# Graph message passing on one core: the column ramp of the one-hot compare moves from a PSUM bank to SBUF

## The reference, cut to what matters

```python
# nodes: 12500 x 64, edges: 200000; row, col = source and destination of each edge (col is sorted)
msg_in = concatenate([nodes[row], nodes[col], edge_features], axis=-1)   # 64 + 64 + 32
messages = relu(msg_in @ mW1 + mb1) @ mW2 + mb2
aggregated = segment_sum(messages, col, num_segments=12500)
upd = relu(concatenate([nodes, aggregated]) @ uW1 + ub1) @ uW2 + ub2
out = layernorm(nodes + upd)
```

## Time and profile before

| | |
|---|---|
| time, median of 3 runs | 1975.1 us (1973.61 to 1975.39) |
| time of the profiled execution | 1975.1 us |
| its span, first to last instruction | 1973.4 us |
| PE busy | 1430.3 us, 72% |
| POOL busy | 1437.8 us, 73% |
| DVE busy | 1066.4 us, 54% |
| ACT busy | 782.8 us, 40% |
| mean granted TensorE clock | 0.802 of full speed |

### The profile page before, as it was taken

The page is one execution under the profiler, slowest core; times in us unless marked ns, Lnnn a source line. Parts: engine busy times, 40 slices in busy tenths (PEclk is TensorE's granted clock), DMA queues, the critical chain, the costliest instruction groups (busy, mean ns, idle before and its releaser), DMA issues.

```text
span 1973.4 us, 41684 instructions
## 1 busy us (share of the span) xinstructions
PE 1430.3 (72%) x10176; PEld 1296.3 (66%) x10176; DVE 1066.4 (54%) x4914; ACT 782.8 (40%) x4005; POOL 1437.8 (73%) x1528
## 2 busy tenths in 40 slices
PE   5777676677676767777676778777777777776776
PEld 5776666666666766666676667666666666675664
DVE  3565455545545545544455555555555656555563
ACT  3353333333333333433333444444444444444442
POOL 1677777777777777777777777777777777777773
PEclk8897878877777787777868787888888787878887
DMA  9833233223322322332232323333322333232321
GB/s 215 241 98 82 79 79 82 80 76 82 82 79 77 84 81 79 78 84 78 77 79 79 80 77 81 79 81 79 81 79 78 81 82 81 77 81 79 81 78 44
DMA packets 173605, 171.32 MB, mean 87 GB/s; under 512 B 72074, under 2 KB 135954, under 8 KB 173474
## 3 DMA queue, kind: packets, MB, share of 16 engines
q0 software_dynamic: 48480, 99.38, 19.4%
q1 hardware_dynamic: 111394, 64.27, 11.7%
q10 hardware_dynamic: 13698, 7.28, 1.6%
HBM read 154.44 MB, written 16.34 MB: 87 GB/s over the span
## 4 chain that ended last, share of the span: by engine, by line
POOL 69%; issue 23%; DMA 3%; PE 2%; POOLq 1%; DVE 1%; SPq 0%; ACT 0%; DVEq 0%; ACTq 0%
POOL ag L314 69%; PE bank L477 1%; DMA src_table<-ag 1%; DMA dst_table<-picks 1%; DMA xc<-x_t 1%; POOLq L233 1%; PE bank L353 0%; POOLq L311 0%; PE bank L368 0%; DVE hid L416 0%; DVE own_x L290 0%; DMA ag<-src_table,slot_idx 0%; DMA own_columns<-resid 0%; PE bank L749 0%; DVE picks L498 0%
## 5 line engine op out<-in xcount | busy, mean ns | idle before, releaser
L314 POOL DMA_INDIRECT ag<-src_table,slot_idx x1515 | 1431.2, 945 | 509.8 <-issue 460.1
L368 PE MATMUL bank<-oh,hid 128*128 128x96 f32 x3128 | 540.1, 328 | 356.5 <-ACT hid L394 353.0
L368 PEld LDWEIGHTS bank<-oh,hid 128*128 128x128 f32 x3128 | 481.7, 235 | 414.0 <-ACT hid L394 401.4
L416 DVE TENSOR_TENSOR hid<-bank,ag 128x512 f32<-128x512 f32 (+1 forms) x391 | 263.7, 674 | 770.6 <-DMA ag<-src_table,slot_idx 752.3
L394 ACT ACTIVATE hid<-hid 128x512 f32<-128x512 f32 x343 | 215.8, 629 | 983.5 <-DVE hid L416 983.5
L353 PE MATMUL bank<-picked,picks 128*128 128x128 f32 x3128 | 567.6, 339 | 7.0 <-DMA picks<-edge_t 6.2
L353 PEld LDWEIGHTS bank<-picked,picks 128*128 128x128 f32 x3128 | 506.5, 245 | 11.9 <-issue 9.2
L302 ACT ACTIVATE own_x<-xc 64x4 uint8 x3072 | 328.3, 189 | 0.0
L290 DVE COPY own_x<-xc 64x4 uint8 x3072 | 305.2, 183 | 12.0
L402 DVE TENSOR_TENSOR oh<-bank,rel 128x384 f32<-128x384 f32 x391 | 217.9, 557 | 54.2 <-issue 25.5
L383 ACT ACTIVATE picks<-bank 96x512 f32<-96x512 f32 x391 | 224.5, 574 | 22.9 <-DMA dst_table<-picks 22.2
(11 more groups left out here) (62 smaller groups left out, 411.3 us busy)
## 6 DMA issues: line engine op xcount, KB each, us to landing
picks<-edge_t SPq DMA_DIRECT2D x391, 64.0 KB
ag<-src_table,slot_idx POOLq DMA_INDIRECT x1515
picked<-dst_table SPq DMA_DIRECT2D x391, 48.0 KB
src_table<-ag SPq DMA_DIRECT2D x25, 256.0 KB, 4.3
dst_table<-picks SPq DMA_DIRECT2D x17, 256.0 KB, 4.5
xc<-x_t ACTq DMA_DIRECT2D x8, 400.0 KB, 15.3
resid<-x_rows SPq DMA_DIRECT2D x24, 128.0 KB
out<-resid ACTq DMA_DIRECT2D x24, 128.0 KB
```

The source lines that it names most:

```text
L314: pool.indirect_dma_start(out=ag[:, k, j * DH:(j + 1) * DH], out_offset=None, in_=src_table, in_offset=bass.IndirectOffsetOnAxis(ap=slot_i ...
L368: nc.tensor.matmul(ps_a[q][:, 0:WIN], hid[:, q, j * DH:(j + 1) * DH], oh[:, r, j * WIN:(j + 1) * WIN], start=(j == 0), stop=(j == TPG - 1))
L416: dve.tensor_tensor(hid[:, q, 0:w], ps_h[q][:, 0:w], ag[:, k, 0:w], ALU.add).then_inc(s_pre, 1)
```

## The change

`iota` gets an SBUF tensor of its own, 96 float32 numbers in each partition, where it was the head of PSUM bank 6. L1059 writes it there, and L402 reads it there. Nothing else of the program is edited, and each engine's instructions stand in the same order as before.

```diff
@@ -92,6 +92,7 @@
         iota_i = sb("iota_i", [P, WIN], i32)
+        iota = sb("iota", [P, WIN])
         ones_bf = sb("ones_bf", [P, P], bf16)
@@ -152,7 +153,6 @@
         ps_h, ps_o, ps_a = banks[0:2], banks[2:4], banks[4:6]
-        iota = banks[6][:, 0:WIN]
@@ -1056,7 +1056,7 @@
             dve.wait_ge(s_iota, 3)
-            dve.tensor_copy(iota, iota_i[:, :])
+            dve.tensor_copy(iota[:, :], iota_i[:, :])
             dve.tensor_copy(trash_f[:, :], trash_i[:, :])
```

## The result

| | before | changed |
|---|---|---|
| median of 4 runs | 1974.89 us (1973.61 to 1975.39) | 1991.68 us (1991.02 to 1992.42) |
| ratio | | 1.0086, 95% interval 1.0068 to 1.0104 |
| profiled execution, its span | 1975.1, 1973.4 us | 1988.31, 1986.6 us |

The change costs 17 us. The forecast was a loss of 45.5 us, 2020.6, and its range began at 2003.0. The direction and the place are as forecast, the size is less than half. The profiled execution lies 3.4 us under the median of the runs, so what follows accounts for 13.2 us and not for 17.

What follows compares the result with a forecast made beforehand. POOL's back-to-back gathers were taken to bound the kernel. L402's shorter duration counted 0 and its 228 collisions 45.5 us, so 1975.1 + 45.5 = 2020.6 us, range 2003 to 2040.

Steps and rivals of the forecast that it cites:

- What bounds the kernel: POOL's back-to-back gathers, 1515 periods of 1.248 us; only a longer POOL instruction or gap changes the time, one for one.
- L402's own duration: DVE's compare L402, 557 ns, gets 0 to 21 ns shorter, 0 to 8.2 us in all; taken as 0.
- What two SBUF inputs do to POOL: A two-SBUF-input DVE instruction running 126 ns into a gather holds POOL to its end: 228 hits, 45.5 us.
- Rival A: No collision from L402, since overwriting the tensor being read is what holds POOL; 1975.1 us, chance 0.06.
- the overlay: The collision rule laid over the trace before, for each of 391 L402: 228 hits and 45.5 us.
- Phases: L402's starts against POOL's gathers stay as they are when delays feed back, since L290 too goes with POOL.
- rival C: Delays avoid each other: lagging POOL meets L402 between read points, all 156 regular hits become misses; 1996.1 us, chance 0.08.
- The prediction's own table of shifts: Loss if L402 moves against POOL: 35.8 us for 104 ns earlier, 58.0 for 104 later, 79.4 for 200.
- the regular 156 hits: L402 starting 950 to 1000 ns after a gather's start, behind L290, all hit; 24.5 us together.
- B: Faster: DVE sets the landing-to-landing rhythm somewhere and L402's 21 ns come off 391 times; 1966.9 us, chance 0.02.
- D: Worse phases: L402 some 100 ns later against the gathers, 2033 us; with 200 ns, 2054.5; chance 0.07.
- Feedback: A delayed gather moves its group's landing and all that follows together; POOL has next to no waits to hide it.

Runs made afterwards that it cites:

- the added wait: Changed kernel (iota in SBUF) with L402 made to wait by a semaphore for the end of the last L290: 2029.16 us, ratio 1.0275 to the kernel before.
- the early-L402 trace: Changed kernel (iota in SBUF) with L402 for group g + 3 moved ahead of the eight L290, behind L434: 2030.39 us, ratio 1.0270.
- The unused tensor's trace: Kernel before (iota in PSUM) plus an unused 96-column SBUF tensor where the changed kernel has iota, moving later tensors by 384 bytes: 1972.89 us, one run.

## Why the prediction was wrong, by its own steps

*What bounds the kernel.* Right. POOL's gap stayed, its instruction grew, and the span grew by the same.

*L402's own duration.* Taken at 557 ns out of 536 to 557; it is 545 (539 to 546 where it starts before the last L290 has ended, 557 and more behind L778 and L802). The reason was not the memory of the operand: the exchange of L433 and L434 gives 545 with iota in PSUM, and the added wait 558 with iota in SBUF.

*What two SBUF inputs do to POOL.* Right in kind and in size: 85 of 91 cases within 15 ns, against 228 cases before with no delay. Rival A, the overwriting of a tensor, is refuted, since L402 writes `oh`. One half of the law was missing. The prediction said that an instruction "that is running at that point holds it", and had no case that started from 44 ns before to 121 ns after a gather's start with which to see that POOL can come first. With the border of 45 ns from the early-L402 trace, the overlay on the trace of before gives 199 hits and 31.6 us, not 228 and 45.5. This corrected overlay is used below. That part of the miss, 13.9 us, is an estimate: the border was measured where L402 starts after the instruction ahead has ended. In the changed kernel 13 L402 that start from 42 ns before to 69 ns after a gather's start still delay it in full, all of 540 to 543 ns. Twelve of them start while L770 runs, which has two SBUF inputs and began ahead of the gather, and the one at 69 ns while an L290 runs. Six that start 15 to 121 ns after it, all of 557 ns or more and none with an instruction still running ahead, don't. An early start by itself is not the reason: in the trace of L402 behind L416, one starts 50 ns after a gather's start while L416 runs, which has one input in PSUM, and the gather takes 947 ns. The likely reading is that DVE, once it has what POOL needs, keeps it when the next such instruction starts before the last has ended. It is not shown: in the trace with the added wait one L402 starts behind L770, 1 ns after a gather's start, and is itself stretched to 589 ns.

*Phases.* This is the step that failed: "phases stay as they are; L290 too goes with POOL", and, against rival C, "L402 follows the end of L290". It followed that end because its PSUM operand started on another partition than the last PSUM read, and the change took this operand away. The change removed the hold, and with it the tie to L290's end.

The sequence: 31.6 us by the corrected overlay (an estimate) at the old phases, 13.8 us measured at the new ones. By what stands ahead of L402 it splits unevenly: 27.1 to 1.6 us where L290 ends less than 300 ns ahead (291 cases), 0.3 to 8.3 behind L770, 4.2 to 3.6 behind L778 and L802. So the early start nearly freed the regular groups and created a new loss behind L770. That the start does it, and not another rhythm of the changed kernel, its own trace shows: with the 316 L402 that start right behind L290, L770 or L434 put back to 31 ns after that instruction's end, the corrected overlay on it gives 194 hits and 29.9 us (an estimate too); as it ran, the same overlay gives 72 hits and 8.0 us, and the rest of the 13.8 is mostly the late starts behind L770. The unused tensor's trace, with 16.9 us, warns that another execution with the hold could have given less than 31.6.

Put back to a later start, the same program loses 53.6; the corrected overlay on the trace of before, shifted by 127 ns (158 instead of 31 ns behind L290), gives 52.5, and on the trace with the unused tensor 30.9. The prediction's own table of shifts shows that it had the lever and did not ask what could pull it: 35.8 us for 104 ns earlier, and the regular 156 hits all rest on margins of 150 ns. (Its 79.4 us for 200 ns later is the value for 208; for 200 the overlay gives 77.0.)

*The rivals.* C named the outcome, regular hits that turn into misses, at 1996.1 us, and gave it 0.08. That it came within 5 us of the time is in part luck: it left 21.0 us at scattered places, and the measured 13.8 stand mostly behind L770. Its reason (a lagging POOL meets L402 elsewhere) is not what happened: the shift is there with iota in PSUM and no collisions. B and D did not occur. The range ended above the result since its lower end was put between C and the forecast.

*Feedback.* That delays shift landings and all that follows together is consistent with the waited version, where the shifted overlay (52.5 us) meets the measured 53.6; no run tests it by itself.

## What to carry to other kernels

When an operand moves to another memory, three things change for its instruction: whom it shares a port with, what it may start before, and so its place against everybody else's rhythm. Price the collision from the trace, but before laying it over the old starts ask what each start hangs on, here the end or the start of the instruction ahead, and whether the edit touches that. Where an engine of short periodic instructions sets the time, a neighbour's cost depends on a few tens of nanoseconds of phase: the same operands cost 17, 54, 55 or 15 us here by place alone.

## What the runs showed of the hardware that was not expected

- A DVE instruction that is not held starts 70 to 73 ns after the start of an L290 ahead (290 of 291); a held one 30 to 33 ns after its end; one behind a semaphore on that end mostly 154 to 161 ns after it.
- The hold can be removed without moving any operand, by the order of two earlier instructions (L434 ahead of L433).
- Which side waits at the shared port depends on who is first. An L402 of two SBUF inputs that starts after the instruction ahead has ended, and 45 ns or more ahead of a gather, keeps POOL waiting to its end; one that starts later costs POOL nothing (126 of 127), and waits itself to 588 to 591 ns after the gather's start (47 cases). One that starts while L770 still runs kept POOL waiting even from 19 to 46 ns after the gather's start (10 cases).
